# Second feed-forward: its norm, turns and routing done chunk by chunk beside the chunk in front

## The reference

```python
x = x + tanh(g_xattn[1]) * L1_xattn(layernorm(x), ctx_2048, ctx_2048, mask, ...)
# L1_ffn on xt = layernorm(x): 8 experts of width 176, the best 2, and a shared one of 176
scores = sigmoid(xt @ gate_w.T)
top_scores, top_idx = top_k(scores, 2)
top_scores = top_scores / (sum(top_scores) + 1e-20) * 2.5
combine = sum(one_hot(top_idx) * top_scores)
routed = einsum('etd,te->td', (silu(xt@w1[e]) * (xt@w3[e])) @ w2[e], combine)
x = x + tanh(g_ffn[1]) * (routed + silu(xt @ sw1) * (xt @ sw3) @ sw2)
```

## Time and profile before

| | |
|---|---|
| median of 3 runs | 1698.78 us (1698.15 to 1702.68) |
| profiled execution, its own time | 1697.2 us |
| its span on the core | 1695.4 us |
| busy in the span | PE 1500.9, DVE 1270.9, ACT 1033.5, POOL 824.3 us |
| last DVE operation of `attention1` ends | 1428.34 us |
| first matmul of `feed_forward` starts | 1460.75 us |
| last DVE operation of `feed_forward` ends | 1692.42 us |

### The profile page before, as it was taken

One profiled execution on the slowest core, in us unless ns is written; L12 is line 12 of the kernel. 1 busy time (PEld: TensorE's weight loads), 2 busy tenths in 40 slices (PEclk: granted clock), 3 DMA queues, 4 the chain that ended last, 5 costly groups with the idle time before them and its releaser, 6 DMA issues. The chain is left out here.

```text
span 1695.4 us, 40055 instructions
## 1 busy us (share of the span) xinstructions
PE 1500.9 (89%) x11666; PEld 1162.7 (69%) x11666; DVE 1270.9 (75%) x4601; ACT 1033.5 (61%) x3244; POOL 824.3 (49%) x1254
## 2 busy tenths in 40 slices
PE   0589999999999999999768879997799997799998
PEld 0489888988889888989644447775566665355554
DVE  5589999999999999999768556664688884544454
ACT  4578888788888888778543435554477774222222
POOL 0766666666666666666314754443566661000000
PEclk9999999999999999999969989999899997799999
DMA  7594300000000000000023634442422200000000
GB/s 299 158 224 109 69 0 0 0 0 0 0 0 0 0 0 0 0 0 1 1 83 100 211 119 122 127 122 89 139 61 72 67 28 3 1 13 1 12 12 12
DMA packets 75227, 95.59 MB, mean 56 GB/s; under 512 B 32138, under 2 KB 60298, under 8 KB 73606
## 3 DMA queue, kind: packets, MB, share of 16 engines
q1 hardware_dynamic: 68278, 75.53, 15.7%
q0 software_dynamic: 6864, 19.01, 3.1%
HBM read 62.74 MB, written 40.43 MB: 61 GB/s over the span
## 5 line engine op out<-in xcount | busy, mean ns | idle before, releaser
L665 ACT ACTIVATE prob<-bS,ntop 128x128 f32<-128x128 f32 x512 | 186.2, 419 | 4.6 <-DVE ntop L474 4.4
L569 POOL TENSOR_TENSOR rs<-ve,half 128x6 f32<-128x6 f32 x128 | 176.8, 1381 | 0.0
L649 ACT COPY pT<-bP 128x512 f32<-128x512 f32 x128 | 75.6, 591 | 144.8 <-PE bP L331 144.8
L577 POOL TENSOR_SCALAR kv<-kv,rs,nb 128x128 f32<-128x128 f32 x256 | 150.4, 593 | 27.5 <-POOL nb L572 27.3
L451 DVE SCALAR_TENSOR_TENSOR qn<-qn,mv,rs 128x128 f32<-128x128 f32 x512 | 155.7, 364 | 6.6 <-POOL rs L569 5.1
L322 PE MATMUL bS<-kT,qT 128*128 128x128 f32 x1024 | 138.2, 278 | 10.8 <-ACT prob L665 10.8
L298 PE MATMUL bq<-w,xq 128*128 128x256 f16 x1024 | 135.0, 276 | 6.6 <-DVE xq L423 6.6
L636 ACT ACTIVATE qT<-bqT,vecs 128x256 f32<-128x256 f32 x256 | 134.6, 594 | 2.5 <-PE bqT L282 2.4
L322 PEld LDWEIGHTS bS<-kT,qT 128*128 128x128 f32 x1024 | 126.0, 194 | 14.0 <-issue 12.7
L339 PE MATMUL bO<-pT,kv 128*128 128x256 f32 x512 | 132.4, 381 | 1.6 <-ACT pT L649 1.6
L356 PE MATMUL bY<-wproj,catq 128*128 128x256 f16 x1024 | 132.7, 273 | 0.8 <-DVE catq L494 0.8
(11 more groups left out here) (296 smaller groups left out, 4307.7 us busy)
## 6 DMA issues: line engine op xcount, KB each, us to landing
f_xblk<-by_slot SPq DMA_DIRECT2D x79, 132.0 KB, 2.1
by_slot<-zeros SPq DMA_DIRECT2D x1, 10112.0 KB, 36.5
l_back<-by_pick SPq DMA_DIRECT2D x16, 512.0 KB, 3.5
f_wstage<-by_expert SPq DMA_DIRECT2D x16, 480.0 KB
l_piece<-in_f_w SPq DMA_DIRECT2D x16, 312.0 KB, 2.9
wo_stage<-in_wproj SPq DMA_DIRECT2D x8, 512.0 KB, 4.2
by_expert<-in_f_w SPq DMA_DIRECT2D x18, 128.0 KB, 2.8
x<-in_x SPq DMA_DIRECT2D x1, 2048.0 KB, 8.5
```

The source lines that it names most:

```text
L569: nc.gpsimd.tensor_tensor(rs[:, t, :], ve[:], r["half"][:, 0:6], ALU.pow).then_inc(rs_ready, 1)
L577: done = nc.gpsimd.tensor_scalar(key, key, rs[:, t, 4 + j:5 + j], nb[:, t, j:j + 1], ALU.mult, ALU.add)
L665: done = nc.scalar.activation(prob[:, t, h, :], bS[:, h, :], ACT.Exp, bias=ntop[:, t, h:h + 1], accum_out=total[:, t, h:h + 1])
```

## The change

`ChunkRouter` takes the place of the block `f1_n`. It does the same steps for one chunk of four batches at a time, with a single bank and single buffers, and its calls are set between the steps of other work on each engine. Chunk 0's calls stand in the steps of `attention1` for b = 14, 15 and 16, where the row statistics of batches 0 to 3 have long been taken; it uses the bank `bx` there. The calls for chunk c + 1 stand between the tiles of chunk c in `feed_forward`. That block is now written out over all 52 tiles without a loop, down tiles always run two behind, also over a chunk's end, and `add_result(c - 1)` stands at tile 1 of chunk c. `bw` has one bank instead of two, and the other is the router's `bx`. `sel` is loaded at the start of `attention1`. In POOL's list the scales of batches 0 to 3 stand before `block_keys(B - 1, 1)`, and that before `split_piece(B // 2 - 1, 0)`. The softmax branch and the other options of `normalise` that no call uses are gone; the first layer's instructions are the same.

```diff
+class ChunkRouter:
...
+    def dve_moments(self, dve, part, some):
...
+        for b in range(part.start, part.stop):
+            done = self.nc.vector.bn_aggr(self.mv[:, b, :], self.r["row_stats"][:, b, :])
+        done.then_inc(self.s["moments"], 1)
...
+    def pool_scales(self, pool, part, some):
+        pool.wait_ge(self.s["moments"], some + 1)
+        self.nc.gpsimd.tensor_tensor(self.ve[:, part], self.mv[:, part, 1], self.r["eps16"][:, part],
+                                     ALU.add).then_inc(self.s["ve_r"], 1)
+        pool.wait_ge(self.s["ve_r"], some + 1)
+        self.nc.gpsimd.tensor_tensor(self.rs[:, part], self.ve[:, part], self.r["half"][:, part],
+                                     ALU.pow).then_inc(self.s["rs_r"], 1)
+
+    def dve_norm(self, dve, c, p):
+        dve.wait_ge(self.s["rs_r"], min(c, 1) + 1)
+        reach(dve, self.s["turned"], 2 * c + p)
+        for j in range(2):
+            b = c * CH + 2 * p + j
+            done = self.nc.vector.tensor_scalar(self.xn[:, j, :], self.r["x"][:, b, :], self.mv[:, b, 0:1],
+                                                self.rs[:, b:b + 1], ALU.subtract, ALU.mult)
+        done.then_inc(self.s["normed"], 1)
...
+    def pe_turn(self, pe, c, p, bank):
+        reach(pe, self.s["low"], 2 * c + p)
+        reach(pe, self.s["shares_r"], c)
+        pe.wait_ge(self.s["normed"], 2 * c + p + 1)
...
+        for j in range(2):
+            for k in range(KT):
+                done = self.nc.tensor.transpose(into[:, k, j, :], self.xn[:, j, k * P:(k + 1) * P], self.r["ident"])
+        done.then_inc(self.s["turned"], 1)
...
+    def pe_logits(self, pe, c, bank):
+        NL, xT, gw = self.q["logits"], self.r["xT"], self.q["gate_w"]
+        pe.wait_ge(self.s["low"], 2 * c + 2)
+        pe.wait_ge(self.s["high"], 2 * c + 2)
...
+    def act_logits(self, act, c, bank):
...
+        act.wait_ge(self.s["logits_r"], c + 1)
+        self.nc.scalar.activation(self.logit[:], bank[:, 0:CH * NL].rearrange("p (i n) -> p i n", i=CH), ACT.Copy,
+                                  scale=1.0 / WS).then_inc(self.s["taken"], 1)
+        act.wait_ge(self.s["taken"], c + 1)
+        self.nc.scalar.activation(self.ex[:], self.logit[:], ACT.Exp, scale=-1.0).then_inc(self.s["ex_r"], 1)
...
+    def dve_scores(self, dve, c):
+        E, K, v = self.q["experts"], self.q["picks"], self.nc.vector
+        dve.wait_ge(self.s["ex_r"], c + 1)
+        self.then(dve, v.tensor_scalar(self.den[:], self.ex[:], 1.0, None, ALU.add))
+        self.then(dve, v.reciprocal(self.score[:, :, 0:E], self.den[:]))
+        for i in range(CH):
+            done = v.max(self.best[:, i, :], self.score[:, i, 0:E])
+        self.then(dve, done)
+        self.then(dve, v.memset(self.best[:, :, K:8], -1.0))
+
+    def dve_shares(self, dve, c):
+        E, v = self.q["experts"], self.nc.vector
+        for i in range(CH):
+            done = v.match_replace(self.rest[:, i, :], self.best[:, i, :], self.score[:, i, :], 0.0)
+        self.then(dve, done)
+        self.then(dve, v.tensor_tensor(self.cw[:, :, 0:E], self.score[:, :, 0:E], self.rest[:, :, 0:E], ALU.subtract))
+        self.then(dve, v.tensor_reduce(self.total[:, 0, :], self.cw[:, :, 0:E], AX, ALU.add))
+        self.then(dve, v.tensor_scalar(self.total[:, 0, :], self.total[:, 0, :], 1e-20, None, ALU.add))
+        self.then(dve, v.reciprocal(self.total[:, 1, :], self.total[:, 0, :]))
+        self.then(dve, v.tensor_scalar(self.total[:, 1, :], self.total[:, 1, :], ROUTED_SCALE, None, ALU.mult))
+        self.then(dve, v.tensor_tensor(self.cw[:, :, 0:E], self.cw[:, :, 0:E],
+                                       self.total[:, 1, :].unsqueeze(2).broadcast_to([P, CH, E]), ALU.mult))
+
+    def dve_parts(self, dve, c):
+        v = self.nc.vector
+        reach(dve, self.s["shares_turned"], c)
+        self.then(dve, v.tensor_copy(self.parts[:, :, 0, :], self.cw[:]))
+        self.then(dve, v.tensor_tensor(self.left[:, 0], self.cw[:], self.parts[:, :, 0, :], ALU.subtract))
+        self.then(dve, v.tensor_copy(self.parts[:, :, 1, :], self.left[:, 0]))
+        self.then(dve, v.tensor_tensor(self.left[:, 1], self.left[:, 0], self.parts[:, :, 1, :], ALU.subtract))
+        v.tensor_copy(self.parts[:, :, 2, :], self.left[:, 1]).then_inc(self.s["parts_r"], 1)
...
+    def pe_shares(self, pe, c, bank):
+        pe.wait_ge(self.s["parts_r"], c + 1)
...
+        for i in range(CH):
+            done = self.nc.tensor.transpose(self.of_shares(bank)[:, i, :], self.parts[:, i].rearrange("p a e -> p (a e)"),
+                                            self.r["ident16"])
+        done.then_inc(self.s["shares_turned"], 1)
...
-        bw = [m.ps(f"{tag}_bw{i}", [P, 512], F32) for i in range(2)]
+        bw, bx = m.ps(f"{tag}_bw", [P, 512], F32), m.ps(f"{tag}_bx", [P, 512], F32)
...
+                reach(pe, hid_done, n)
+                if j == 0:
+                    pe.wait_ge(router.s["shares_r"], c + 1)
+                cw_rows = cwT[:].rearrange("e b s -> e (b s)")[:, c * CH * S:(c + 1) * CH * S]
+                nc.tensor.matmul(bw[:], sel[:, j * P:(j + 1) * P], cw_rows, start=True, stop=True).then_inc(w_ready, 1)
...
+            for n in range(N):
+                c, j = divmod(n, NT)
+                up(n)
+                if n >= 2:
+                    down_tile(n - 2)
+                if c + 1 < NC:
+                    if j in (2, 4):
+                        router.pe_turn(pe, c + 1, j // 2 - 1, bx[:])
+                    if j == 6:
+                        router.pe_logits(pe, c + 1, bx[:])
+                    if j == 11:
+                        router.pe_shares(pe, c + 1, bx[:])
+            down_tile(N - 2)
+            down_tile(N - 1)
...
+                if c + 1 < NC:
+                    if j in (3, 5):
+                        router.act_high(act, c + 1, j // 2 - 1, bx[:])
+                    if j == 7:
+                        router.act_logits(act, c + 1, bx[:])
...
+            router.pool_scales(pool, rest, 1)
...
+            router.dve_moments(dve, rest, 1)
+            for n in range(N):
...
+                nc.vector.scalar_tensor_tensor(out=hid[:, t, :], in0=gated[:, t, :], scalar=1.0 / WS, in1=bw[:],
+                                               op0=ALU.mult, op1=ALU.mult).then_inc(hid_done, 1)
+                if j == 1 and c > 0:
+                    add_result(c - 1)
+                if c + 1 < NC:
+                    if j == 1:
+                        router.dve_norm(dve, c + 1, 0)
+                    if j == 3:
+                        router.dve_low(dve, c + 1, 0, bx[:])
+                        router.dve_norm(dve, c + 1, 1)
+                    if j == 5:
+                        router.dve_low(dve, c + 1, 1, bx[:])
+                    if j == 8:
+                        router.dve_scores(dve, c + 1)
+                    if j == 9:
+                        router.dve_shares(dve, c + 1)
+                    if j == 10:
+                        router.dve_parts(dve, c + 1)
+                    if j == 12:
+                        router.dve_take_shares(dve, c + 1, bx[:])
+                reach(dve, down_done, n - 1)
+                dve.wait_ge(high_done, n + 1)
+                nc.vector.tensor_tensor(low[:, t, :], hid[:, t, :], high[:, t, :], ALU.subtract).then_inc(low_done, 1)
...
+                if at_end(b, B - 2, c, 3):
+                    pe.wait_ge(x_low, B)
+                    router.pe_turn(pe, 0, 0, bx[:])
+                if at_end(b, B - 1, c, 1):
+                    router.pe_turn(pe, 0, 1, bx[:])
+                if at_end(b, B - 1, c, 3):
+                    router.pe_logits(pe, 0, bx[:])
+                if at_end(b, B, c, 2):
+                    router.pe_shares(pe, 0, bx[:])
...
+                if at_end(b, B - 1, c, 0):
+                    router.act_high(act, 0, 0, bx[:])
+                if at_end(b, B - 1, c, 2):
+                    router.act_high(act, 0, 1, bx[:])
+                if at_end(b, B, c, 0):
+                    router.act_logits(act, 0, bx[:])
...
-                    nc.vector.bn_stats(r["row_stats"][:, b - 2, :], x[:, b - 2, :])
+                    dve.sem_inc(waited, 1)
+                    nc.vector.bn_stats(r["row_stats"][:, b - 2, :], x[:, b - 2, :]).then_inc(rows_measured, 1)
+                if at_end(b, B - 2, c, 0):
+                    dve.wait_ge(rows_measured, CH)
+                    router.dve_moments(dve, first, 0)
+                if at_end(b, B - 2, c, 2):
+                    router.dve_norm(dve, 0, 0)
+                if at_end(b, B - 1, c, 0):
+                    router.dve_low(dve, 0, 0, bx[:])
+                    router.dve_norm(dve, 0, 1)
+                if at_end(b, B - 1, c, 2):
+                    router.dve_low(dve, 0, 1, bx[:])
+                if at_end(b, B, c, 0):
+                    router.dve_scores(dve, 0)
+                if at_end(b, B, c, 1):
+                    router.dve_shares(dve, 0)
```

(11 more changed lines are left out.)

338 lines of the change are left out of this document (120 added, 218 removed).

## The result

The changed kernel takes **1675.1 us** (median of 4 runs, 1672.83 to 1676.8) against 1698.51 for the kernel before: ratio 0.9844, interval 0.9818 to 0.9871, so 1.6% faster. The forecast was 1671, with 1664 to 1679 as its range. The profiled execution took 1672.83 us (span 1671.1) against 1697.2 (span 1695.4): the span is 24.3 us shorter. Ratios and their intervals are taken over executions at the usual granted clock; of e1's ten executions two (1726.39 and 1730.09 us) and of e11's six one (1762.67 us) ran at a lower one and are left out.

What follows compares the result with a forecast made beforehand. Attention and feed_forward were taken as bound by PE, with 32.4 us between them all on the path. The terms -32.1 - 3.6 + 6.1 + 2.0 = -27.6 us gave 1671 us, range 1664 to 1679.

Steps and rivals of the forecast that it cites:

- The block: Between attention's last row statistics and feed_forward's first matmul: of 32.4 us only a 0.3 us meeting stays, gain 32.1 us.
- The stops: PE's stops of 1.2 us at chunk ends in feed_forward: three of four go, gain 3.6 us.
- one bank couples PE and DVE: Rival: in feed_forward PE's `bw` matmul waits for `hid` in each tile, giving 1704 us or more; chance 0.02.
- no effect: Rival: without loops in feed_forward some engine waits for its own instructions, losing as much as was won, 1699 us; chance 0.01.
- PE's work in the feed-forward: Added transposes, logit matmuls and share transposes on PE count whole: 6.1 us over three chunks, at most 8.4.
- DVE, ACT and POOL in the feed-forward: Added work there fits idle time and the 2.17 us of room before PE needs `bw`: cost nothing.
- Hand-overs cost PE: Rival: PE stops at router calls in feed_forward for late ACT and DVE work, 7 us more, 1678; chance 0.14.
- The table switches: At tile 7 ACT's exponential needs two table loads between two silus, at most 3.14 us; it just fits, cost nothing.
- Attention's tail: Chunk 0's turns, logits and routing in attention's last batches and drain add 2.0 us, between 0.6 and 5.8.
- The signs: Expected in the trace: last statistics about 1430.3, first `bg` 0.3 us behind, turn tiles 5.0 us, no stops between chunks.
- The clock rival: Rival: added PE work in attention's drain keeps the clock at its upper level, some 4 us won, 1667; chance 0.10.

Runs made afterwards that it cites:

- e1: Kernel before with feed_forward's loops written out over all tiles, two banks `bw` and `f1_n` kept, no router calls in the feed-forward: ratio 0.9974 to the kernel before.
- e11: Changed kernel with POOL's last weight pieces behind chunk 0's norms, shares' parts behind the last divide, fifteen filling matmuls: ratio 0.9816 to the kernel before, median 1666.5 us.
- e2: Kernel before with feed_forward's loops written out and a single bank `bw`, `f1_n` kept, no router calls in the feed-forward: ratio 0.9978 to the kernel before.
- e8: Changed kernel with POOL's two last pieces of the weight split held back until chunk 0's two norms are done: ratio 0.9821 to the kernel before.
- e10: Changed kernel with POOL's last weight pieces behind chunk 0's norms, shares' parts behind the last divide, sixteen filling matmuls: ratio 0.982 to the kernel before.
- e7: Changed kernel with four filling matmuls behind attention's last one and fourteen more in the drain's gaps: ratio 0.9818 to the kernel before.

## Why the prediction was right, point by point

- **The block, -32.1.** Measured -32.09, with a meeting of 0.32 us. Right.
- **The stops, -3.6.** Measured -3.49 (e1, e2). Nearly right; and that the single bank and the unrolling cost nothing by themselves is shown by the two, which excludes the rivals "one bank couples PE and DVE" and "no effect".
- **PE's work in the feed-forward, +6.1.** Measured 5.73. The durations of groups overlap what comes next, so a turn was 0.44 and not 0.66; the logits were 0.61 and the share turn 0.43 where I had 0.5 and 0.24 by halving a time of the lower clock. Per chunk that is 0.44 too much and 0.3 too little; that the term came out is in part luck.
- **DVE, ACT and POOL in the feed-forward, 0.** Right: the rest is 214.15 plus PE's own added work. "Hand-overs cost PE" did not come: no router call on PE waits there.
- **The table switches, 0.** The result was right, the working was not, so that was luck as far as the sum goes. The load ahead of silu stands behind a wait, so silu is 1.29 us late and the 2.17 us of room carried it. No drain beside the load appears: the exponential starts 0.02 us after the load ends.
- **Attention's tail, +2.0, bounds 0.6 and 5.8.** Measured +3.37, a term that was undersized. The two turns took 1.09 and 0.44 us, 1.53 where 1.3 was forecast, and 0.65 of it was POOL's interference (e8), which I had not seen: I had asked only whether POOL comes too late. The drain itself grew by 1.84, from 15.27 to 17.11: 0.63 by the router's work ahead of the last products, on DVE and ACT and not by the logits on PE, 1.11 by the clock, which fell earlier and of which I had looked only at the good side, and 0.10 behind. DVE's choice of experts, 4.3 us as forecast, did fit: the divide still waited 1.59 us for PE.
- **The first tiles.** No term of mine. With the turn's 0.44 off they took 0.9 us more than before. The window of 1433.40 to 1440 shows 0.56. This scatters: with the turns taken off it is 11.6 to 13.2 in the kernels without filling.
- **A drift of 1.4 us** ahead of the change, which is the scatter of the executions.
- **The signs.** The first `bg` was 0.32 us behind the last statistics (0.3 named), no router call made PE wait in the feed-forward, and no stop was left between chunks. But tiles with a turn took 4.76 us and not 5.0, the last statistics ended at 1433.08 and not 1430.3, from first `bg` to the last down matmul it was 3.15 us more and not 2.5, and of DVE's idle time ahead of the last `divide` 1.59 us remained.

Together -32.09 - 3.49 + 5.73 + 3.37 + 0.90 + 1.37 = -24.2, the span's -24.3. The forecast -27.6 was 3.4 too good: 1.4 drift, 1.4 tail, 0.9 start and 0.1 stops, less 0.4 of PE's work. Leaving out the drift, which is no part of the mechanism, the sum was 2.0 us off in the profiled execution.

**The clock rival** was right as a lever and wrong as a result of this change: the added work did not hold the clock (0.63). Fifteen or sixteen matmuls more did, together with the new order and POOL's edit (e10, e11); eighteen without these two did not (e7). The page "TensorE: Matmul & The Clock Gate" of the Trainium skill, in Part 1, says that activity releases the throttle; the fillings of e11, with the clock at 1.00, agree.

What stays open: with how few fillings the clock stays up in the new order, since only fifteen and sixteen were tried there; and why the clock falls at a different place in the drain from one execution to the next.

## What to carry to other kernels

A serial block of small operations between two PE-bound stages can be cut into chunks and laid beside them. Here the 32.1 us that went cost 5.7 of PE's own work in the feed-forward, read from start to start, 3.4 in the tail and 0.9 at the start, so about two thirds stayed. Give each hidden piece the number at which it stops being hidden (here `hid`'s 2.17 us at the single bank), because beyond it the price can be more than the wait. When one engine of a chain gets faster, look at once at what its former slowness covered: put what the chain needs (the divide) ahead of what merely has to be done.
